# A decoder layer on one core: where TensorE does the first half of the down projection within a step of the pairs' stage

## The reference

```
h = x + scan(x) @ wo
x1 = layernorm(x + h + silu(rms(h) @ wg) * (rms(h) @ wu) @ wd)
x2 = layernorm(x1 + (softmax(q(x1) @ k(ctx).T / 4) @ v(ctx)) @ Wo + bo)
out = layernorm(x2 + expert[argmax(x2 @ Wr + br)](x2))
```

## Time and profile before

| | us |
|---|---|
| median of three runs | 1915.34 |
| lowest and highest | 1914.19, 1918.46 |
| the profiled execution | 1919.56 |
| its span from the first to the last instruction | 1917.4 |
| mean granted TensorE clock | 0.859 |

### The profile page before, as it was taken

The page is one execution under the profiler, slowest core; times in us unless marked ns, Lnnn a source line. Parts: engine busy times, 40 slices in busy tenths (PEclk is TensorE's granted clock), DMA queues, the critical chain, the costliest instruction groups (busy, mean ns, idle before and its releaser), DMA issues. The chain is left out here.

```text
span 1917.4 us, 28138 instructions
## 1 busy us (share of the span) xinstructions
PE 1369.9 (71%) x6660; PEld 939.9 (49%) x6661; DVE 1199.3 (63%) x3351; ACT 756.6 (39%) x2416; POOL 1007.4 (53%) x1246
## 2 busy tenths in 40 slices
PE   6514558500047667668757999996599999999997
PEld 4413446400035555556546677775355555555554
DVE  4499999999988999999772235344232323222222
ACT  5521225401123766667864688885111111111110
POOL 3258998886679998898666323421111111121211
PEclk9857779855578888888967999997799999999999
DMA  4601114600221011110102112223311401501200
GB/s 123 210 26 34 45 34 142 234 23 0 78 66 32 22 32 39 32 32 17 37 17 88 54 38 63 100 71 123 109 49 62 164 20 37 182 30 62 67 17 6
DMA packets 97684, 125.40 MB, mean 65 GB/s; under 512 B 10001, under 2 KB 74952, under 8 KB 95560
## 3 DMA queue, kind: packets, MB, share of 16 engines
q1 hardware_dynamic: 60040, 97.22, 15.7%
q10 hardware_dynamic: 33136, 18.58, 3.3%
q0 software_dynamic: 4432, 8.73, 1.3%
HBM read 89.68 MB, written 35.74 MB: 65 GB/s over the span
## 5 line engine op out<-in xcount | busy, mean ns | idle before, releaser
L239 POOL TENSOR_TENSOR wt<-wt 128x1024 f32<-128x1024 f32 x128 | 301.5, 2356 | 46.7 <-DVE wt L184 31.9
L245 POOL TENSOR_TENSOR wt<-wt 128x512 f32<-128x512 f32 (+2 forms) x384 | 307.2, 800 | 30.1
L1868 PE MATMUL e_ph<-wt,e_g 128*128 x624 | 274.3, 592 | 0.0
L184 DVE SCALAR_TENSOR_TENSOR wt<-wt,scan 128x256 f32<-128x256 f32 x512 | 241.5, 472 | 1.8 <-POOL wt L239 1.7
L163 DVE TENSOR_REDUCE wt<-wt 128x16 f32<-128x272 f32 x512 | 218.8, 427 | 0.1
L174 DVE TENSOR_TENSOR scan<-wt,scan 128x256 f32<-128x256 f32 x512 | 214.7, 419 | 0.3
L152 DVE TENSOR_TENSOR wt<-wt,scan 128x256 f32<-128x256 f32 x512 | 209.6, 409 | 0.5 <-PEq L262 0.5
L1359 ACT ACTIVATE wt<-p_pX,p_mx 128x120 f32<-128x120 f32 x512 | 176.9, 389 | 75.0 <-DVE p_mx L1146 74.9
L1761 POOL TENSOR_TENSOR e_ve<-e_mv,eps 128x1 f32<-128x1 f32 x39 | 7.5, 191 | 368.7 <-DVE e_mv L1812 368.7
L1491 PE MATMUL p_pm<-p_w_mix,p_oT 128*128 128x256 f32 x128 | 43.9, 502 | 197.8 <-DMA p_oT<-o 168.1
L1868 PEld LDWEIGHTS e_ph<-wt,e_g 128*128 128x128 f32 x624 | 115.5, 190 | 130.8 <-issue 130.8
(11 more groups left out here) (223 smaller groups left out, 2879.4 us busy)
## 6 DMA issues: line engine op xcount, KB each, us to landing
wt<-in_L_ffn_W SPq DMA_DIRECT2D x24, 1024.0 KB
qkv<-f_st ACTq DMA_DIRECT2D x48, 256.0 KB, 2.3
p_kE<-kE SPq DMA_DIRECT2D x16, 480.0 KB, 3.6
p_vP<-vP SPq DMA_DIRECT2D x16, 480.0 KB
wt<-qkv SPq DMA_DIRECT2D x6, 1024.0 KB, 9.5
e_xt<-routed ACTq DMA_DIRECT2D x39, 130.0 KB
f_xt<-in_x SPq DMA_DIRECT2D x16, 256.0 KB, 2.9
p_oT<-o SPq DMA_DIRECT2D x16, 256.0 KB
```

The source lines that it names most:

```text
L184: nc.vector.scalar_tensor_tensor(s["S"][:, h, u], s["S"][:, h, (u - 1) % R], s["gate"][:, jb, h, 2, bass.ds(c * R + u, 1)], s["outer"][:], ...
L239: nc.gpsimd.tensor_tensor(x, s["S"][:, h, z * Q:(z + 1) * Q], s["qn"][:, h, z * Q:(z + 1) * Q].rearrange("p t (o d) -> p t o d", o=1).to_b ...
L245: nc.gpsimd.tensor_tensor(x[:, :, :, 0:half], x[:, :, :, 0:half], x[:, :, :, half:2 * half], ALU.add).then_inc(s["o_fold"][h], 1)
L1868: ins = nc.tensor.matmul(ph2[:], g1[:, c // (C1 // 2), c % (C1 // 2)], wt[:, bass.ds(at_b + (W2_AT + c * F2), F2)], start=(c == 0), stop=( ...
```

## The change

In TensorE's step the block of the first two score groups moves behind `down(f, 0)`, with all its waits. No instruction is added or taken away, and no other engine's order is changed. Where f is not on, nothing changes.

```diff
                 if "d" in on:
                     probabilities(d, range(6, 8))
-                if "c" in on:
-                    if "d" in on:
-                        pe.wait_ge(PT_out, d * 8 + 6)
-                    score(c, 0)
-                    if "d" in on:
-                        pe.wait_ge(PT_out, d * 8 + 8)
-                    score(c, 1)
                 if "f" in on:
                     if "c" in on:
                         pe.wait_ge(x1T_out, c + 1)
                     if "e" in on:
                         pe.wait_ge(position, placed(e, PLACED))
                     if since(d, 1):
                         pe.wait_ge(x2T_out, d)
                     down(f, 0)
+                if "c" in on:
+                    if "d" in on:
+                        pe.wait_ge(PT_out, d * 8 + 6)
+                    score(c, 0)
+                    if "d" in on:
+                        pe.wait_ge(PT_out, d * 8 + 8)
+                    score(c, 1)
                 if "d" in on:
                     values(d)
                 if "c" in on:
                     score(c, 2)
```

## The result

The changed kernel takes 1976.65 us in the median of 4 runs (1973.53 to 1979.44), the kernel before 1914.76 us beside it (1913.39 to 1918.46): a ratio of 1.032 with a 95% interval of 1.0298 to 1.0341, or 61.9 us. The forecast was 1958 with a range of 1940 to 1969. The side and the places were right, the size was not. The profiled execution took 1976.48 us with a span of 1974.3, so between the two traces there are 56.9 us; 4.8 us of the 61.9 are that the profiled execution of before lay above its own median and that of after did not. I take the 56.9 apart.

What follows compares the result with a forecast made beforehand. The prediction took DVE to bound steps 3 to 7 and PE steps 15 to 20. Terms of 23.1 + 19.9 = 43 us on the profiled 1919.6 gave 1962.6, or 1958 at the median, range 1940 to 1969.

Steps and rivals of the forecast that it cites:

- the chain in the DVE regime: Steps 3 to 9: scores come later behind the down projection, DVE stalls at its maximum; 20.1 us, 23.1 with the clock.
- The local waits: DVE stalls by step, 3 to 9: 2.05, 0, 5.3, 3.8, 3.8, 2.2 and 3.0 us.
- step 8's wait for the count: Step 8, DVE's 2.51 us wait for the count's matmuls: queries only 0.8 us earlier relative to DVE; step loses 2.2.
- the length of the way to score 2: Steps 16 to 18, from the scores' start to score 2, table load behind the maximum: 6.67 us.
- how much of that way is idle: PE's idle before score 2: near 3 us in steps 16 to 18, 1.2 to 1.5 in 15, 19 and 20.
- a change of form less: Steps 14 to 20, one boundary of the array's form less: at most 0.18 us each, 1.3 in all, not counted.
- the clock's term in the PE regime: Slower PE clock after idle: 1.5 us per step 16 to 18, 0.7 in step 14, nothing in 15, 19, 20; 5.2.
- the stalls: Steps 14 to 20, PE waits for ACT's exponentials before score 2: 14.7 us without the clock.
- The clock holds: Rival, both regimes: same stalls without the clock's 3.0 + 5.2, step 5 at 3.8; 33 us, 1949; chance 0.27.
- More than the sum: Rival: clock also falls in steps 15, 19, 20 and slows scores in 5 to 7; 54 us, 1969; chance 0.1.
- The switch decides: Rival, steps 14 to 20: fewer switches of the array's form win 1.3 us, 2.5 with hidden waits; 1913; chance 0.02.
- Half is absorbed: Rival, steps 3 to 10: DVE's stalls taken back from POOL's backlog and DVE's idle; 14.7 to 27 us, 1936; chance 0.1.

Runs made afterwards that it cites:

- filled_first: New order in steps 0 to 10 only, plus six useless matmuls while PE waits for `position` in steps 5 to 7: 1942.36 us, 1.0132 of the kernel before.
- grouped_behind: Kernel before with `down(f, 0)` moved behind the values, ahead of score 2, in all steps: 1918.25 us, ratio 1.0007.
- filled: second_pass plus six useless matmuls between the values and score 2: 1934.19 us, 1.0095 of the kernel before.
- second_pass: Kernel before with the new order from step 11 on only, the old order in steps 0 to 10: 1944.86 us, ratio 1.0143.

## Why the prediction was right in its mechanism and wrong in size

**Right: the chain in the DVE regime.** Forecast 23.1 us for steps 3 to 9, measured 25.7, of which 1.8 are given back before step 14. That 23.9 are left, so near to the forecast, is partly luck: neither the 1.8 nor the 3.3 of the next paragraph were in the sum. The local waits came out: step 4 nothing, steps 5 and 7 5.50 and 5.54 us of idle, step 8's wait for the count 0.8 us shorter. The clock fell behind 3.6 us of idle and cost 1.66 us (4.64 against 2.98; forecast 1.5).

**A small term not foreseen.** DVE's two-element operation at L1174 took 0.27, 0.67, 0.60 and 0.15 us in steps 5 to 8 before, and 1.12, 1.29, 1.29 and 1.29 after (the row at 832.93 above). That is 3.3 us together, and it explains the 0.6 to 1.1 us by which each of these steps exceeds its idle. The traces show what it ends with: in every row of L1174 above 0.2 us in the traces of before, after and *filled_first*, 18 in all, it ends 0.01 to 0.03 us behind a POOL instruction that was running when it began. At 832.93 that is POOL's 2.36 us at L239, which ends at 834.19, and DVE at 834.22. The operation's price is what was left of POOL's; no run moved POOL's work by itself.

**Right: the length of the way to score 2.** Forecast 6.67 us from the scores' start in the loop steps, measured 6.66 (1178.42 to 1185.08), with ACT's table load behind the maximum in step 16 and ahead of it in step 15, as in the earlier trace rows:

```profile
1138.88 1.28 ACT L1359 ACT_TABLE_LOAD   x1
...
1180.88 1.28 ACT L1359 ACT_TABLE_LOAD   x1 [4.31 <-DVE p_mx L1146]
```

**Wrong in a detail: how much of that way is idle.** I forecast 2.9 us of idle in steps 16 to 18 and 1.2 to 1.5 in steps 15, 19 and 20, since I read the pair of scores as 1.91 us of work. It is 1.04 (1178.42 to 1179.46); in the kernel before it held a wait of 0.87 us for the copies of probability groups 6 and 7, as *grouped_behind* shows, which the profile does not set apart, since the busy ends of matmuls are modelled. The down projection now hides that wait. For the stall it makes no odds, because the wait vanished from one side and appeared on the other: 2.57 us a loop step against 2.9 forecast. But the idle by which the clock had to be judged became 3.67 and 2.23 us instead of 2.9 and 1.3. The 0.18 us which I worked out for a change of form less came from the same misread row and don't follow from it.

**The step that failed: the clock's term in the PE regime.** I took "1.5 us for each loop step (0 to 1.9) and 0.7 for step 14", and for steps 15, 19 and 20 "nothing": 5.2 us. Measured: 3.11 in each loop step, 0.89 + 2.71 in step 14, 1.7 in steps 15 and 19, 0 in step 20, which is 9.3 + 3.6 + 3.4 = 16.3 us, three times the forecast. What is left for the stalls is 11.8 us, 2.9 under the forecast of 14.7; 1 us of this is that step 14 takes so much back in later idle of PE, which I had said these steps don't have. Both together are 28.1 against 19.9, and these 8.2 us are most of the 13.9 by which the profiled execution missed. I had the 1.5 from single blocks, the down projection of step 5 and the eight matmuls behind 2.24 us of idle in step 21. I noted that those behind them ran slow too (the next score group takes 1.97 us instead of 1.08), and left them out of the price. The whole stretch until the first matmul at full clock belongs to it, here two blocks.

**The rest of the miss** is mostly outside the changed steps: 1.5 us before the change is reached, 2.4 in steps 21 to 23 (1.1 of it in step 21's queries, 3.40 us where they took 2.32, and 0.9 in its output projection, 3.69 where it took 2.83), 1.0 in the experts. No run here parts it from the scatter between executions. And I deducted 4.2 us to go from the profiled execution to the median, which the new kernel's runs don't have.

**Rivals.** "The clock holds" is refuted by *filled*. "More than the sum" had the right kind of cause (more of the clock, in steps 15, 19 and 20) and its 1969 was nearest. It held for steps 15 and 19, which is 3.4 of the 11.1 us that the clock's term lacked; 4.8 are in the loop steps and 2.9 in step 14. Its other half, slower scores in steps 5 to 7, did not occur (they take 1.04 us). "The switch decides" needed the exponentials of group 0 within 3.8 us of the scores' start; they took 6.66, and the 0.3 us a step that one change less may be worth stand against 2.57 of stall. "Half is absorbed" is seen for a small part: the 1.8 us between steps 9 and 14. The Trainium skill, "TensorE: Matmul & The Clock Gate", section "HAM oscillation", was cited in the prediction for the rule that gaps make each burst start at the low clock. The traces agree for the 3.67 us of idle in steps 16 to 18, where score group 2 itself takes 1.97 us. Behind 2.23 us in steps 15 and 19 the burst starts at full clock (score group 2 in 1.08) and falls only in the down projection, and in step 20 it doesn't fall at all.

## What to carry to other kernels

Before a block is moved on a busy engine, ask what it covered where it stood: here 2.98 us of down projection hid a chain through two other engines, and moving it changed no instruction and cost 3%. An idle on TensorE is to be priced twice, as a wait and as the stretch at half clock behind it, followed block by block until the durations are those of full clock; behind 1.4 to 4.1 us of idle that stretch cost 0 to 3.6 us here, in places more than the wait. If a block has to be moved partly, find the wait that it can fill ahead and leave behind what the chain needs as cover: two matmuls of six, with the table load moved off the chain, gave the 0.24% that neither gave alone.

## What the runs showed of the hardware that was not expected

- The clock's price is not a function of the idle alone: 1.45 us of idle cost 0 or 1.65 us, 2.39 us cost 1.6 to 3.2, in iterations of one loop of one execution.
- Adding six matmuls of no use to each step made the kernel 10.7 us faster (*filled* against *second_pass*).
- A wait of 0.87 us stood inside a merged row of matmuls as busy time (1.91 against 1.04 us for the same pair of score groups).
- A DVE operation on 128x2 elements (L1174) took between 0.13 and 1.29 us (2.13 in one case of the trace before); wherever it took more than 0.2 us it ended 0.01 to 0.03 us behind a POOL instruction that was running when it began.
- The table load costs the 1.28 us of its row and nothing beside it: the idle went from 3.67 to 2.39 and from 1.45 to 0.17 when it was moved. The Trainium skill, "ScalarE: Activation LUTs", section "What ACT_TABLE_LOAD costs", adds a drain of about the same length to each switch. These runs show none on this way: in step 16 of the changed kernel the load ends at 1182.16 and the first exponential starts at 1182.18, where ACT had been idle for 4.31 us in front of the load.
